# Half of the last stage's joins and norms done on TensorE, ScalarE and GpSimd during the scan (a fused gated block, Trainium2)

## The chip, the cores and the metric

The kernel runs on one core of one Trainium2 chip, as one launch. The metric is the device time of that launch in microseconds; the runs shown are separate executions of the same program. A profile of one further execution gives the trace.

## What is computed

The reference is a chain of four gated pairs, each an attention-like step and a feed-forward step on a residual `x` of 8 batches x 256 tokens x 256 features. The change touches only the last pair:

```python
x = x + tanh(g_xattn[3]) * scan(layernorm(x), ctx)     # _L3_xattn_ref
x = x + tanh(g_ffn[3]) * bit_ffn(layernorm(x), ...)    # _L3_ffn_ref

# scan, for each token t in order, from W = ctx (256 x 256 for each batch), lr = 1/256:
y_t = sigmoid(W @ x_t)
W   = W + lr * (outer(y_t, x_t) - (y_t ** 2)[:, None] * W)

# bit_ffn: ternary weights, activations rounded to 8 bits by the largest |value| of each token
gate = silu(bitlinear(x, w_gate)); up = bitlinear(x, w_up); out = bitlinear(gate * up, w_down)
```

A token's output of the scan depends on all tokens before it. The feed-forward step works on each token alone, so it can start on a token as soon as the scan has passed that token.

## The kernel before

`x` is held in SBUF as 16 row tiles of 128 tokens x 256 features (`core.x`, in profiles `x_res`), two for each batch: tile 2b holds tokens 0 to 127 of batch b, tile 2b+1 tokens 128 to 255. `core.xn` (`x_norm`) holds the normalised rows in the same form.

**The scan** (`scan_steps`, line 2923) runs over 256 tokens in order, all 8 batches at once, with the features on the partitions. W is never formed: the products of tokens with each other are computed before the loop, and for each token VectorE forms the next input `v` from small operations on 16 to 96 columns (lines 3009, 3015, 3046, 3089 and, at the third token of a group of four, 3061 to 3070). ScalarE turns `v` into `y` (line 2983, kept in `y_all`, feature by token) and writes a second copy (line 2987); VectorE cannot go on to the next token's square (line 3024) before that. Tokens form 64 groups m of four (i = 0 to 3). After each group TensorE turns the group's values (line 3148), ScalarE copies them out at i = 1 of the next group (line 2992), TensorE adds products to the accumulators `acc` (lines 3116, 3125), and fills up with idle passes on the identity matrix (line 3134) to a fixed number of passes for each group. GpSimd has nothing to do in this loop. An engine runs its instructions in the order in which its program lists them.

**The last stage** (`stage_tail`, line 3176) takes the 16 row tiles through a pipeline written out by hand: each engine runs turns u = 0 to 23, and in turn u each step works on tile u minus its own lag. The order inside a turn is the order of the `at(...)` calls. The steps, with engine and line of the profile:

- `turn_y` (TensorE, 3242) turns `y_all` to row form; `join` (VectorE, 223 with `tanh_g`) adds it to `x`; `stats` and `mean_var` (VectorE, 3420, 3424); `rstd` (GpSimd, 182 and 185); `normalise` (VectorE, 217).
- `x_range`, `x_cut`, `x_inverse` (VectorE, 3377, 3382, 3386) give the scale of the rounding; `x_scales` (GpSimd, 3449 to 3455); `scale_x` (ScalarE, 3313); `turn_x` (TensorE, 3251); `copy_x` (ScalarE, 3320) takes the turned tile out of PSUM.
- `gate_product` and `up_product` (TensorE, 3261); `gate_silu` (ScalarE, 3329); `product` (VectorE, 3395); `h_range`, `h_scale`, `h_inverse` (VectorE, 3400, 3406, 3411); `h_scales` (GpSimd, 3460, 3462); `scale_h` (ScalarE, 3338); `turn_h` (TensorE, 3279); `copy_h` (ScalarE, 3346); `down` (TensorE, 3289); `leave` (VectorE, 223 with `bt_gate`) adds the result to `x`, and SyncE stores the tile.

`turn_y` and `down` share one PSUM bank. The lags are 0 for the join, 1 for normalise and x_range, 3 for turn_x and copy_x, 4 for the gate and up products, 5 for product and h_range, 6 for turn_h, 7 for down and leave.

`Chain.link` (line 48) gives an instruction a semaphore and makes the engine wait for it before the next one.

## Time and profile before

| | us |
|---|---|
| median of 3 runs | 2042.1 (2037.2 to 2042.43) |
| the profiled execution, its own time | 2038.59 |
| its span in the trace | 2036.9 |
| the scan's loop, start of token 0 to last `y` | about 1669 to 1942 |
| the last stage | about 1943 to 2037 |
| TensorE / VectorE / ScalarE / GpSimd busy over the span | 1865.6 / 1262.3 / 828.5 / 275.4 |

Busy time counts an engine's instructions from start to end, and instructions that follow each other overlap by their latency, so a stretch in which an engine is busy all the time is one in which it never ran dry; how long an instruction keeps the next one waiting is read from start to start. The last 1.7 us between span and time lie outside the trace.

### The profile page before, as it was taken

What the parts mean: (1) busy time and instruction counts of PE and PEld (TensorE: products, weight loads), DVE (VectorE), ACT (ScalarE), POOL (GpSimd) and SP (SyncE); (2) the same over time, 40 slices, a digit from 0 to 9 for tenths busy, and PEclk for the clock granted to TensorE, in tenths of its full rate; (3) what the DMA queues carried; (4) which work ended last, traced back from release to release, by engine and by line L of the source; (5) the groups of instructions that cost most, each with busy time, mean ns of one, the idle gap of its engine ahead of it and who ended that gap; (6) DMA issues with size and microseconds to landing.
All of it is one profiled execution on the core that took longest, in us unless ns stands there. A gap on an engine that the chain in (4) does not pass through costs nothing. (4 is left out here: it accounts for less than half of the span.)

```text
span 2036.9 us, 38837 instructions
## 1 busy us (share of the span) xinstructions
PE 1865.6 (92%) x13683; PEld 1512.2 (74%) x13708; DVE 1262.3 (62%) x4621; ACT 828.5 (41%) x2246; POOL 275.4 (14%) x498
## 2 busy tenths in 40 slices
PE   8899999999998998999999998997983989999978
PEld 6567766777666998999999997776542877777745
DVE  7868876877884361111111145676797539999988
ACT  3434335555563111111111111774486424444468
POOL 2001112000001070000000044332000320000032
PEclk9999999999999998999999999899995989999989
DMA  6211111121112622222222012111000031111100
GB/s 229 89 55 52 43 51 73 46 80 42 42 42 64 244 73 88 88 85 86 87 88 85 23 55 65 45 46 36 29 0 1 0 106 35 36 38 39 24 11 33
DMA packets 106724, 124.98 MB, mean 61 GB/s; under 512 B 36160, under 2 KB 85832, under 8 KB 104776
## 3 DMA queue, kind: packets, MB, share of 16 engines
q1 hardware_dynamic: 95704, 107.64, 15.8%
q0 software_dynamic: 3072, 8.39, 1.3%
q10 hardware_dynamic: 7792, 6.95, 1.0%
q8 instruction: 87, 1.43, 0.3%
q14 instruction: 69, 0.57, 0.1%
HBM read 86.39 MB, written 36.63 MB: 60 GB/s over the span
## 5 line engine op out<-in xcount | busy, mean ns | idle before, releaser
L1804 DVE TENSOR_TENSOR me_h<-me_sg,me_ps_u 128x512 f32<-128x512 f32 x106 | 72.8, 687 | 281.7 <-PE me_ps_u L1615 265.7
L1756 ACT ACTIVATE me_sg<-me_ps_g 128x512 f32<-128x512 f32 x106 | 63.3, 597 | 372.6 <-PE me_ps_g L1615 339.9
L1276 ACT ACTIVATE ca_e<-ca_scored,ca_neg_max 128x256 f32<-128x256 f32 x256 | 127.2, 499 | 108.6 <-DVE ca_neg_max L1335 108.6
L1615 PE MATMUL me_ps_g<-me_x_turned,me_w 128*128 128x128 f32 x1184 | 145.8, 277 | 1.9 <-issue 1.9
L1615 PEld LDWEIGHTS me_ps_g<-me_x_turned,me_w 128*128 128x128 f32 x1184 | 142.1, 193 | 4.3 <-issue 2.1
L1615 PE MATMUL me_ps_u<-me_x_turned,me_w 128*128 128x128 f32 x1184 | 144.5, 275 | 0.0
L1623 PE MATMUL me_ps_y<-me_w,me_h 128*128 128x256 f32 x592 | 140.0, 379 | 0.0
L1615 PEld LDWEIGHTS me_ps_u<-me_x_turned,me_w 128*128 128x128 f32 x1184 | 138.4, 192 | 0.0
L2983 ACT ACTIVATE sc_y_all<-ss_v 128x16 f32<-128x16 f32 x256 | 60.9, 238 | 156.5 <-DVE ss_v L3046 156.4
L1623 PEld LDWEIGHTS me_ps_y<-me_w,me_h 128*128 128x128 f32 x592 | 106.8, 190 | 11.4
L1335 DVE CUSTOM_DVE_ANT_0 ca_scored<-ca_main,ca_mask_add 128x256 f32<-128x256 f32 x256 | 93.0, 422 | 21.5 <-PE ca_main L1219 21.5
L2434 PE MATMUL ig_ps<-nw_int_wT,x_norm 128*128 128x512 f32 (+1 forms) x256 | 90.2, 497 | 0.3 <-ACT if_up L2490 0.3
L3015 DVE SCALAR_TENSOR_TENSOR ss_left<-ss_nq,ss_v 128x16 f32<-128x16 f32 x446 | 90.5, 203 | 0.0
L3134 PE MATMUL ss_idle<-ident 128*128 128x128 f32 x648 | 90.1, 285 | 0.0
L2009 POOL DMA_INDIRECT me_rows<-moe_y_list,me_slot x32 | 31.3, 979 | 429.2 <-DVE carrier L81 421.3
L3134 PEld LDWEIGHTS ss_idle<-ident 128*128 128x128 f32 x648 | 79.4, 195 | 6.3 <-issue 3.2
L2213 ACT ACTIVATE la_e<-la_scores,la_mx 128x128 f32<-128x128 f32 x256 | 70.4, 423 | 33.3 <-DVE la_mx L2255 33.3
L1828 DVE COPY me_y<-me_ps_y 128x256 f32<-128x256 f32 x37 | 15.7, 425 | 108.0 <-PE me_ps_y L1623 108.0
L1231 PE MATMUL ca_turned<-ident,ca_e 128*128 128x128 f32 x512 | 69.3, 279 | 10.6 <-DVE ca_e L1348 10.6
L1231 PEld LDWEIGHTS ca_turned<-ident,ca_e 128*128 128x128 f32 x512 | 57.0, 142 | 27.1 <-DVE ca_e L1348 19.4
L1348 DVE TENSOR_SCALAR ca_e<-ca_e,ca_rsums 128x256 f32<-128x256 f32 x256 | 74.6, 356 | 2.3
L2434 PEld LDWEIGHTS ig_ps<-nw_int_wT,x_norm 128*128 128x128 f32 x256 | 47.1, 194 | 34.0 <-issue 31.7
(451 smaller groups left out, 4365.6 us busy)
## 6 DMA issues: line engine op xcount, KB each, us to landing
me_w<-in_L_ffn_w_e SPq DMA_DIRECT2D x24, 1024.0 KB, 7.7
ca_k_list<-kv_out SPq DMA_DIRECT2D x28, 256.0 KB, 2.3
ca_v_list<-kv_out SPq DMA_DIRECT2D x28, 256.0 KB, 2.3
sk_gb<-scan_g_band SPq DMA_DIRECT2D x14, 512.0 KB, 3.7
moe_x_list<-me_zeros SPq DMA_DIRECT2D x1, 5248.0 KB, 21.8
me_x_tile<-moe_x_list SPq DMA_DIRECT2D x38, 128.0 KB, 2.0
moe_y_list<-me_y ACTq DMA_DIRECT2D x37, 128.0 KB, 1.7
ca_kT<-ca_k_list SPq DMA_DIRECT2D x4, 1024.0 KB, 4.8
```

Source lines behind the costliest of these rows:

```text
L1231: last = nc.tensor.transpose(ps[:, jt * S + it * P:jt * S + (it + 1) * P], e[:, g % 3, e_, it, jt * P:(jt + 1) * P], core.ident[:, :])
L1276: nc.scalar.activation(e[:, g % 3, e_, it, :], scored[:, g % 2, e_, it, :], ACT.Exp, scale=-1.0, bias=neg_max[:, g % 2, n:n + 1], accum_ou ...
L1335: last = nc.vector.tensor_tensor_reduce(scored[:, g % 2, e_, it, :], ps[:, it * S:(it + 1) * S], mask_add[:, b, :], -1.0, -NEG, ALU.add, A ...
L1348: last = nc.vector.tensor_scalar(e[:, g % 3, e_, it, :], e[:, g % 3, e_, it, :], rsums[:, par, n:n + 1], None, ALU.mult)
L1615: last = nc.tensor.matmul(ps[:, j * P:(j + 1) * P], w[:, n, kt, f:f + P], x[:, kt, :], start=(kt == 0), stop=(kt == KD - 1))
L1623: last = nc.tensor.matmul(ps_y[:, 0:D], h[:, c, j, :], w[:, f, :], start=(f == 0), stop=(f == FT - 1))
L1756: nc.scalar.activation(sg[:, c, :], ps_g[c][:, :], ACT.Silu).then_inc(done, 1)
L1804: nc.vector.tensor_tensor(h[:, c, :, :].rearrange("p j n -> p (j n)"), sg[:, c, :], ps_u[c][:, :], ALU.mult).then_inc(done[c], 1)
L2213: last = nc.scalar.activation(e[:, n % 2, r, j, :], scores.ps[r][:, j * P:(j + 1) * P], ACT.Exp, bias=mx[:, n % 2, r, j:j + 1])
L2434: last = nc.tensor.matmul(ps[t % 2][:, lo:hi], xT[:, t, kt * P:(kt + 1) * P], wT[:, w, kt, lo:hi], start=(kt == 0), stop=(kt == KD - 1))
L3015: return nc.vector.scalar_tensor_tensor(out, nq[:, t % 2, :].unsqueeze(2).broadcast_to([P, C, n]), 1.0, src, ALU.add, ALU.mult)
L3134: nc.tensor.matmul(idle[:, 0:P], core.ident[:, :], core.ident[:, :], start=True, stop=True)
```

## The change

The eight tiles that hold tokens 0 to 127 (tile 2b of each batch) are joined and normalised while the scan runs over tokens 128 to 255. It is done in four rounds of two tiles, started at groups 33, 37, 41 and 45. In a round, TensorE turns four 128x128 blocks of `y_all` into a new PSUM bank `ps_f` (`turn_front`), taking the place of four idle passes; ScalarE copies the bank, scaled by `tanh_g`, to a part of SBUF that an earlier stage used (`joined`), after the third token of the group behind; and GpSimd adds it to `x`, takes the mean by folding each row in halves, subtracts it, takes the variance in the same way, and scales: 23 instructions, each waiting for the one before. From the second round on ScalarE's copy also waits until GpSimd is through with the round before.

In the last stage the tiles come in a new order, `tile(t)`: first the eight that are ready, then the other eight. The steps turn_y, join, stats, mean_var, rstd and normalise are done for t = 8 to 15 alone (`at_rest`); the turns begin with u = 1; and `copy_x` goes from ScalarE to VectorE, where it stands behind `leave`.

```diff
@@ -2926,6 +2926,7 @@
     PER = TB // TG
     C = KD * B
     SENT = NG - 2
+    FRONT = tuple(NG // 2 + 1 + 4 * j for j in range(B // 2))
     PASSES = 28
     QUARTER = (0, 1, 0, 1, 2, 3, 0, 1, 0, 1, 2, 3, 0, 1, 2, 3)
     with ExitStack() as ctx:
@@ -2942,6 +2943,12 @@
         ps_z = [st.ps(f"ps_z{j}", [P, 512]) for j in range(2)]
         acc = [st.ps(f"acc{j}", [P, KD, 512]) for j in range(2)]
         idle = st.ps("idle", [P, 512])
+        ps_f = st.ps("ps_f", [P, 2, KD, P])
+        int_wT = core.next_weights.int_wT
+        joined = int_wT[:, 0, 0, 0:2 * D].rearrange("p (n d) -> p n d", n=2)
+        folded = int_wT[:, 0, 1, 0:2 * P].rearrange("p (n k) -> p n k", n=2)
+        mean, rstd = st.sb("mean", [P, 2, 1]), st.sb("rstd", [P, 2, 1])
+        f_ps, f_read, front = st.sem("f_ps"), st.sem("f_read"), Chain(st.sem("front"), 23)
         gb_in = [st.sem(f"gb_in{j}") for j in range(2)]
         gm_in = [st.sem(f"gm_in{n}") for n in range(NBLK)]
         v_ready, y_ready, yz_ready, z_ready = (st.sem(n) for n in ("v_ready", "y_ready", "yz_ready", "z_ready"))
@@ -2991,6 +2998,13 @@
                     act.wait_ge(z_ps, m)
                     nc.scalar.activation(zT[rows, k, :, :].rearrange("p h n -> p (h n)"),
                                          ps_z[(m - 1) % 2][rows, 0:KD * P], ACT.Copy).then_inc(zT_ready, 1)
+                if i == 2 and m - 1 in FRONT:
+                    j = FRONT.index(m - 1)
+                    act.wait_ge(f_ps, j + 1)
+                    if j >= 1:
+                        act.wait_ge(front.sem, front.per * j)
+                    nc.scalar.activation(joined, ps_f[:, :, :, :].rearrange("p n h k -> p n (h k)"), ACT.Copy,
+                                         scale=core.tg[:, 3:4]).then_inc(f_read, 1)
 
         @block.vector
         def _(dve):
@@ -3133,6 +3147,15 @@
                 for _ in range(passes // 2):
                     nc.tensor.matmul(idle[:, 0:P], core.ident[:, :], core.ident[:, :], start=True, stop=True)
 
+            def turn_front(j):
+                pe.wait_ge(y_ready, S // 2)
+                if j >= 1:
+                    pe.wait_ge(f_read, j)
+                for n in range(2):
+                    for h in range(KD):
+                        last = nc.tensor.transpose(ps_f[:, n, h, :], y_all[:, h, 2 * j + n, 0:P], core.ident[:, :])
+                last.then_inc(f_ps, 1)
+
             start_block(0)
             start_block(1)
             for m in range(SENT):
@@ -3170,7 +3193,36 @@
                 for s in share[early:]:
                     whole(ahead, s)
                 real = 12 + 4 * len(share[early:]) + (4 if g < 2 and k + 1 < NBLK else 0)
+                if m in FRONT:
+                    turn_front(FRONT.index(m))
+                    real += 4
                 busy(max(0, PASSES - real))
+
+        @block.gpsimd
+        def _(pool):
+            def fold(link, wide, out):
+
+                link(nc.gpsimd.tensor_tensor(folded[:, :, :], wide[:, :, 0:P], wide[:, :, P:D], ALU.add))
+                n = P // 2
+                while n > 1:
+                    link(nc.gpsimd.tensor_tensor(folded[:, :, 0:n], folded[:, :, 0:n], folded[:, :, n:2 * n], ALU.add))
+                    n //= 2
+                link(nc.gpsimd.tensor_tensor(out, folded[:, :, 0:1], folded[:, :, 1:2], ALU.add))
+
+            for j in range(B // 2):
+                link = front.turn(pool, j).link
+                x, xn = core.x[:, 4 * j:4 * j + 3:2, :], core.xn[:, 4 * j:4 * j + 3:2, :]
+                pool.wait_ge(f_read, j + 1)
+                link(nc.gpsimd.tensor_tensor(x, x, joined[:, :, :], ALU.add))
+                fold(link, x, mean[:, :, :])
+                link(nc.gpsimd.tensor_scalar(mean[:, :, :], mean[:, :, :], 1.0 / D, None, ALU.mult))
+                link(nc.gpsimd.tensor_tensor(xn, x, mean[:, :, :].broadcast_to([P, 2, D]), ALU.subtract))
+                link(nc.gpsimd.tensor_tensor(joined[:, :, :], xn, xn, ALU.mult))
+                fold(link, joined[:, :, :], rstd[:, :, :])
+                link(nc.gpsimd.tensor_scalar(rstd[:, :, :], rstd[:, :, :], 1.0 / D, LN_EPS, ALU.mult, ALU.add))
+                link(nc.gpsimd.tensor_tensor(rstd[:, :, :], rstd[:, :, :],
+                                             core.minus_half[:, :].unsqueeze(1).broadcast_to([P, 2, 1]), ALU.pow))
+                link(nc.gpsimd.tensor_tensor(xn, xn, rstd[:, :, :].broadcast_to([P, 2, D]), ALU.mult))
 
 
 def stage_tail(nc, core, ins, y_all):
@@ -3211,31 +3263,45 @@
         ha_ready, h_ps, hT_ready = st.sem("ha_ready"), st.sem("h_ps"), st.sem("hT_ready")
         out_ps, x_done, stored = st.sem("out_ps"), st.sem("x_done"), st.sem("stored")
         X_SMALL, H_SMALL = 4, 2
-        LAST = 8
+        FIRST, LAST = 1, 8
+        AHEAD = TILES // 2
         block = ctx.enter_context(nc.Block())
 
         def turns(eng_turn):
-            for u in range(TILES + LAST):
+            for u in range(FIRST, TILES + LAST):
                 eng_turn(u)
 
         def at(step, t):
             if 0 <= t < TILES:
                 step(t)
+
+        def at_rest(step, t):
+
+            if AHEAD <= t < TILES:
+                step(t)
+
+        def tile(t):
+
+            return 2 * t if t < AHEAD else 2 * (t - AHEAD) + 1
+
+        def rest(t):
+
+            return t - AHEAD
 
         @block.sync
         def _(sp):
             outs = core.out.rearrange("b (h p) d -> p (b h) d", p=P)
             for t in range(TILES):
                 sp.wait_ge(x_done, t + 1)
-                sp.dma_start(outs[:, t, :], core.x[:, t, :]).then_inc(stored, 16)
+                sp.dma_start(outs[:, tile(t), :], core.x[:, tile(t), :]).then_inc(stored, 16)
             sp.wait_ge(stored, 16 * TILES)
 
         @block.tensor
         def _(pe):
             def turn_y(t):
-                b, half = divmod(t, 2)
-                if t >= 1:
-                    pe.wait_ge(y_added, t)
+                b, half = divmod(tile(t), 2)
+                if rest(t) >= 1:
+                    pe.wait_ge(y_added, rest(t))
                 if t >= 7:
                     pe.wait_ge(x_done, t - 6)
                 for h in range(KD):
@@ -3282,7 +3348,8 @@
 
             def down(t):
                 pe.wait_ge(hT_ready, 2 * t + 2)
-                pe.wait_ge(y_added, min(TILES, t + 7))
+                if rest(t + 7) >= 1:
+                    pe.wait_ge(y_added, rest(min(TILES, t + 7)))
                 if t >= 1:
                     pe.wait_ge(x_done, t)
                 for f in range(FT):
@@ -3296,7 +3363,7 @@
                 at(down, u - 7)
                 at(turn_h, u - 6)
                 at(up_product, u - 4)
-                at(turn_y, u)
+                at_rest(turn_y, u)
 
             turns(turn)
 
...
-            def copy_x(t):
-                act.wait_ge(x_ps, t + 1)
...
-                at(copy_x, u - 3)
...
+            def copy_x(t):
+                dve.wait_ge(x_ps, t + 1)
+                if t >= 2:
+                    dve.wait_ge(up_ps, 2 * (t - 1))
+                nc.vector.tensor_scalar(xT[:, t % 2, :, :].rearrange("p k n -> p (k n)"), ps_x[:, 0:D], MAGIC, None,
+                                        ALU.subtract).then_inc(xT_ready, 1)
+
             def join(t):
-                dve.wait_ge(y_ps, t + 1)
-                residual(nc, dve, core, tg, ps_yo[:, 0:D], t, y_added)
+                dve.wait_ge(y_ps, rest(t) + 1)
+                residual(nc, dve, core, tg, ps_yo[:, 0:D], tile(t), y_added)
 
             def normalise(t):
-                norm.vector_apply(dve, t, t % 2)
+                dve.wait_ge(norm.rstd_ready, rest(t) + 1)
+                nc.vector.tensor_scalar(core.xn[:, tile(t), :], core.x[:, tile(t), :], norm.mv[:, t % 2, 0:1],
+                                        norm.rstd[:, t % 2:t % 2 + 1], ALU.subtract, ALU.mult).then_inc(norm.done, 1)
 
             def x_range(t):
-                dve.wait_ge(norm.done, t + 1)
-                nc.vector.tensor_reduce(xmax[:, t:t + 1], core.xn[:, t, :], AX.X, ALU.max, apply_absolute_value=True
+                if t >= AHEAD:
+                    dve.wait_ge(norm.done, rest(t) + 1)
+                nc.vector.tensor_reduce(xmax[:, t:t + 1], core.xn[:, tile(t), :], AX.X, ALU.max, apply_absolute_value=True
                                         ).then_inc(xmax_ready, 1)
 
...
             def turn(u):
                 at(product, u - 5)
                 at(leave, u - 7)
+                at(copy_x, u - 3)
                 at(h_range, u - 5)
-                at(normalise, u - 1)
+                at_rest(normalise, u - 1)
                 at(h_scale, u - 5)
                 at(x_range, u - 1)
                 at(h_inverse, u - 5)
-                at(join, u)
+                at_rest(join, u)
                 at(x_cut, u - 1)
-                at(stats, u)
+                at_rest(stats, u)
                 at(x_inverse, u - 1)
-                at(mean_var, u)
+                at_rest(mean_var, u)
...
```

How the order of the instructions moves: first TensorE in the scan, group m = 33 (`ss_ps_f` is the new PSUM bank, `ss_idle` the idle passes; the line numbers of the change are higher). Before:

```order
L3116 MATMUL ss_acc<-sk_gm,ss_zT 128x128 x2
L3125 MATMUL ss_acc<-sk_gm,ss_zT 128x8x4 x2
L3125 MATMUL ss_acc<-sk_gm,ss_zT 128x128 x2
L3134 MATMUL ss_idle<-ident 128x128 x6
L3148 MATMUL ss_ps_z<-ident,ss_z 32x128 x2
```

And with the change:

```order
L3130 MATMUL ss_acc<-sk_gm,ss_zT 128x128 x2
L3139 MATMUL ss_acc<-sk_gm,ss_zT 128x8x4 x2
L3139 MATMUL ss_acc<-sk_gm,ss_zT 128x128 x2
L3156 MATMUL ss_ps_f<-ident,sc_y_all 128x128 x4
L3148 MATMUL ss_idle<-ident 128x128 x4
L3171 MATMUL ss_ps_z<-ident,ss_z 32x128 x2
```

The four transposes stand behind the group's products, and two idle multiplications (four passes) are gone.

ScalarE beside it, with the change (`nw_int_wT` is the SBUF part that holds `joined`); before, the same rows stand there without L3006:

```order
L2999 ACTIVATE ss_zT<-ss_ps_z 32x256
L2990 ACTIVATE sc_y_all<-ss_v 128x16
L2994 ACTIVATE ss_az<-ss_v 128x16
L3006 ACTIVATE nw_int_wT<-ss_ps_f,tanh_g 128x512
L2990 ACTIVATE sc_y_all<-ss_v 128x16
L2994 ACTIVATE ss_az<-ss_v 128x16
```

The copy stands between the third and the fourth token of the group: the fourth token's `y` is queued behind it.

VectorE in the last stage, one full turn before (u = 7 and later), from leave on:

```order
L223 SCALAR_TENSOR_TENSOR x_res<-bt_ps_yo,bt_gate,x_res 128x256
L3400 TENSOR_REDUCE bt_hmax<-bt_hp 128x1
L217 TENSOR_SCALAR x_norm<-x_res,bt_ln_mean_var,bt_ln_rstd 128x256
L3406 TENSOR_SCALAR bt_hsc<-bt_hmax,bt_cgu 128x1
L3377 TENSOR_REDUCE bt_xmax<-x_norm 128x1
```

and with the change the same place for u = 7, the last turn without join and norm:

```order
L3465 TENSOR_TENSOR bt_hp<-bt_sg,bt_ps_u 128x512 x2
L223 SCALAR_TENSOR_TENSOR x_res<-bt_ps_yo,bt_gate,x_res 128x256
L3432 TENSOR_SCALAR bt_xT<-bt_ps_x 128x256
L3470 TENSOR_REDUCE bt_hmax<-bt_hp 128x1
L3476 TENSOR_SCALAR bt_hsc<-bt_hmax,bt_cgu 128x1
L3447 TENSOR_REDUCE bt_xmax<-x_norm 128x1
L3481 RECIPROCAL bt_hinv<-bt_hsc 128x1
L3452 TENSOR_SCALAR bt_xs<-bt_xmax 128x1
L3456 RECIPROCAL bt_xr<-bt_xs 128x1
```

The norm has left the turn, and the copy out of PSUM (L3432) has come into it; from u = 8 on the join and its statistics, and from u = 9 on the norm, are back, and the copy stays.

## Rows read from the trace of the kernel before

**Rows 1.** Stretches: length; PE, PEld, DVE, ACT, POOL busy us (count); PEclk; DMA share; GB/s.
```profile
1696.90:1917.90 221.00, 205.66 (x1460) 169.61 (x1460) 216.93 (x1610) 93.69 (x467) 0.00 (x0) 1.00 0.15 37
1971.05:2008.16 37.11, 34.82 (x222) 22.49 (x225) 37.11 (x106) 37.11 (x66) 13.88 (x64) 1.00 0.09 30
```
**Rows 2.** Timeline around group 33: start us, us, engine, line, form, idle before.
```profile
1817.55 0.22 ACT L2987 ACTIVATE ss_az<-ss_v 128x16 f32<-128x16 f32 x1
...
1818.32 1.60 PE L3134 MATMUL ss_idle<-ident 128*128 128x128 f32 x12
1818.42 0.24 ACT L2983 ACTIVATE sc_y_all<-ss_v 128x16 f32<-128x16 f32 x1 [0.65 <-DVE ss_v L3046]
...
1818.70 0.19 DVE L3024 SCALAR_TENSOR_TENSOR ss_nq<-sc_y_all 128x16 f32<-128x16 f32 x1
```
**Rows 3.** Timeline of GpSimd: a wide addition undisturbed, small operations of the last stage.
```profile
324.90 0.72 POOL L1378 TENSOR_TENSOR x_res<-x_res,kv_bias 128x256 f32 x1
2004.73 0.19 POOL L3450 TENSOR_TENSOR bt_xs<-bt_xs,bt_amax_inv 128x1 f32<-128x1 f32 x1
2005.00 0.19 POOL L3452 TENSOR_TENSOR bt_cgu<-nw_bit_scale,bt_xs 128x2 f32<-128x2 f32 x1
2005.68 0.55 POOL L185 TENSOR_TENSOR bt_ln_rstd<-bt_ln_rstd,minus_half 128x1 f32<-128x1 f32 x1
```
**Rows 4.** VectorE line 1348, 128x256 from SBUF to SBUF: beside GpSimd, alone, and beside it in time.
```profile
L1348 DVE TENSOR_SCALAR ca_e<-ca_e,ca_rsums x4: 347/348/353, 421.0 to 421.8; 128x256 f32<-128x256 f32 x4
326.43 0.82 DVE L1348 TENSOR_SCALAR ca_e<-ca_e,ca_rsums 128x256 f32<-128x256 f32 x1
327.17 0.81 DVE L1348 TENSOR_SCALAR ca_e<-ca_e,ca_rsums 128x256 f32<-128x256 f32 x1
```
**Rows 5.** A small GpSimd operation beside VectorE operations on two SBUF tensors (timeline), and its group.
```profile
146.53 0.74 POOL L182 TENSOR_TENSOR f_ln_rstd<-f_ln_mean_var,eps 128x1 f32<-128x1 f32 x1 [12.02 <-DVE f_ln_mean_var L176]
146.36 0.86 DVE L671 SCALAR_TENSOR_TENSOR f_qh_down<-f_qh_above,f_qh_up 128x704 f32<-128x704 f32 x1
L182 POOL TENSOR_TENSOR f_ln_rstd<-f_ln_mean_var,eps x14: 742/744/746, 146.5 to 302.5; 128x1 f32<-128x1 f32 x14
```
**Rows 6.** Timeline of the start of the last stage, the steps on the way to the first product.
```profile
1943.56 0.21 DVE L3365 TENSOR_SCALAR bt_c_out<-tanh_g,nw_bit_scale 128x1 f32<-128x1 f32 x1
1947.94 0.15 DVE L3386 RECIPROCAL bt_xr<-bt_xs 128x1 f32<-128x1 f32 x1
1949.86 0.47 ACT L3320 ACTIVATE bt_xT<-bt_ps_x,bt_magic 128x256 bf16<-128x256 f32 x1 [0.78 <-PE bt_ps_x L3251]
1953.56 1.49 PE L3261 MATMUL bt_ps_g<-nw_bit_wT,bt_xT 128*128 128x512 bf16 x3 [0.22 <-issue]
1954.84 1.87 PE L3261 MATMUL bt_ps_u<-nw_bit_wT,bt_xT 128*128 128x512 bf16 x4
1958.78 1.27 DVE L3395 TENSOR_TENSOR bt_hp<-bt_sg,bt_ps_u 128x512 f32<-128x512 f32 x2
```
**Rows 7.** VectorE in the last stage: the groups of the four moved steps, and two timeline rows.
```profile
L223 DVE SCALAR_TENSOR_TENSOR x_res<-bt_ps_yo,tanh_g,x_res 128x256 f32<-128x256 f32 x16 | 7.5, 470 | 0.3 <-PE bt_ps_yo L3242 0.3
L3420 DVE BATCH_NORM_STATS2 bt_ln_stats<-x_res 128x6 f32<-128x256 f32 x16 | 6.8, 427 | 0.0
L217 DVE TENSOR_SCALAR x_norm<-x_res,bt_ln_mean_var,bt_ln_rstd 128x256 f32<-128x256 f32 x16 | 6.5, 408 | 5.8 <-POOL bt_ln_rstd L185 5.8
L3424 DVE BATCH_NORM_AGGREGATE bt_ln_mean_var<-bt_ln_stats 128x2 f32<-128x6 f32 x16 | 2.9, 182 | 0.0
1984.97 0.47 DVE L223 SCALAR_TENSOR_TENSOR x_res<-bt_ps_yo,tanh_g,x_res 128x256 f32<-128x256 f32 x1
1985.35 0.14 DVE L3382 TENSOR_SCALAR bt_xs<-bt_xmax 128x1 f32<-128x1 f32 x1
```
**Rows 8.** ScalarE's turn of the last stage, timeline around the copy that moves.
```profile
1991.42 0.45 ACT L3320 ACTIVATE bt_xT<-bt_ps_x,bt_magic 128x256 bf16<-128x256 f32 x1
1991.78 1.25 ACT L3329 ACTIVATE bt_sg<-bt_ps_g,bt_cgu 128x512 f32<-128x512 f32 x2
```

21 lines of the change are left out of this document (9 added, 12 removed).

## The prediction

> **What bounds the kernel now.** The busy time by stretch comes first, since the change has two places. In the scan's loop VectorE is busy for 216.93 of 221.00 us, ScalarE for 93.69, GpSimd not at all [rows 1]; 52 groups of four tokens pass in that stretch, 4.25 us each. VectorE alone sets this pace. In the last stage's full turns VectorE and ScalarE are both busy all the time, 37.11 of 37.11 us for eight turns, 4.64 us a turn [rows 1]; there the reader is to see two engines close to the bound. The timeline of the stage's start then shows a long filling: from VectorE's first own operation at 1943.56 to the first product at 1958.78 it takes 15.2 us, in which join, statistics, GpSimd's root and norm follow each other for every tile [rows 6]. VectorE waits 5.8 us for GpSimd's root there [rows 7].
>
> All sums are made against the profiled execution (2038.59). It lies 3.5 us under the median of the three runs and 2.0 under their mean (2040.6); I add the net difference to that mean. From run to run some 0.3% (6 us) is about what a measurement of this kernel can tell from no change.
>
> **The change part by part.**
>
> *The filling gets shorter.* For the first tiles VectorE starts with x_range at once, about 1943.7; x_cut and x_inverse follow within 0.6 us, so x_inverse of tile 0 starts near 1944.3 instead of 1947.94. From there to the copy out of PSUM it took 1949.86 - 1947.94 = 1.9 us [rows 6], so copy_x(0) stands near 1946.2. It lasts 0.47, the second tile's transpose (waiting for it) some 0.7, so gate_product(0) starts near 1947.4. From the gate product to the up product it took 1.28 us [rows 6], and half of the up product's 1.87 is needed: first product near 1949.6 instead of 1958.78. Gain 9.2 us.
>
> *Turns without join and norm.* u = 5 to 7 lose join, stats, normalise and mean_var: durations 470, 427, 408 and 182 ns, each keeping the next one 0.09 us less than it lasts (join: 1985.35 - 1984.97 = 0.38) [rows 7], together 1.13 us. ScalarE loses copy_x, 1991.78 - 1991.42 = 0.36 us [rows 8]; VectorE gets it at about the same 0.36. VectorE's turn would be 4.64 - 1.13 + 0.36 = 3.9, ScalarE's 4.64 - 0.36 = 4.3 at most. Some leaves wait for `down` in these turns; I take 0.5 us of gain for the three.
>
> *Full turns.* u = 8 to 15 keep everything and VectorE, already full, gets copy_x: 8 x 0.36 = 2.9 us lost. The last turns, where ScalarE was late, give back about 0.6. Last stage: -9.2 - 0.5 + 2.9 - 0.6 = **-7.4 us**, between -4 (copy waits for turn_x, filling saves only 6) and -11 (full turns at 4.64, because the copy fills gaps).
>
> *TensorE.* Four transposes stand in place of two idle multiplications. L3134's row of 12 lasts 1.60 us, 0.13 each [rows 2]: four transposes take some 0.55. They can start at 1818.32, where the idle passes begin, and nobody waits for the idle passes: nothing, except as the start of the next point.
>
> *ScalarE's copy in front of a `y`.* ScalarE is free from about 1817.77 (L2987's end) and would wait for the transposes to 1818.95; the copy reads 128x512 from PSUM, as bt_sg does, 1.25 us for two [rows 8], so about 0.6 until the next instruction starts. The fourth token's `y` then starts at 1819.6 instead of 1818.42. Behind it is L3024, which started 0.04 us after that `y` ended [rows 2], and behind that all of VectorE. No slack: 1.2 us a round, **+4.8 us** for four; nothing if the copy somehow slips into a gap, 7 if the transposes come later.
>
> *GpSimd's 23 chained instructions.* A 128x256 addition lasts 0.72 us and a one-column one 0.19 [rows 3], so 2.07 ns a column; a dependent one starts 0.08 us after the end of the one before (2004.73 + 0.19 to 2005.00). A round has four operations of 512 columns and two folds of 256, 128, 64, 32, 16, 8, 4 and 2: 3068 columns, 6.4 us. With 23 x 0.27 and 0.36 more for the power (0.55 against 0.19) a round takes 13.0 us. Rounds begin four groups apart, 17.0 us. They fit, with 4 us to spare, and GpSimd's own time is hidden.
>
> *What GpSimd's operations cost VectorE.* This decides. L1348, 128x256 from SBUF to SBUF, lasts 0.35 us and follows itself every 0.27 us (421.0 to 421.8 for four). Beside GpSimd's 128x256 additions it lasts 0.81 and follows itself every 327.17 - 326.43 = 0.74 us [rows 4]: the two engines take turns, and VectorE loses 0.47 us for each GpSimd operation of 256 columns, two thirds of that operation. Does that hold for the scan's VectorE operations, which mostly read two SBUF tensors and have no such twin here? One direction is seen: a one-column GpSimd operation lasts 0.74 instead of 0.19 us, and ends at 147.27, just behind VectorE's L671 (146.36 + 0.86 = 147.22), an operation on two SBUF tensors; 14 of 14 do so [rows 5]. The two exclude each other then, and I take it that they do in the other order too. At 0.47 us for 256 columns a round's wide operations (4 x 512, 2 x 448) hold VectorE for 5.4 us; the narrow ones (under 64 columns) fit between two VectorE starts and cost nothing; and each of some ten wide ones begins while VectorE could not have started anyway, 0.08 us each. That is 4.6 us a round, **+18.3 us** for four. The bounds are 0 (two-tensor reads are not held) and 4 x 10.8 = 43 (GpSimd's whole durations, 23 x 0.19 + 6.4 a round).
>
> The Trainium skill, "SBUF — State Buffer", section "Who interferes with whom", says that a VectorE instruction with two SBUF inputs contends with a GpSimd instruction that reads SBUF, and that the one that issues second is blocked until the first has finished. The trace agrees for the one order, and its 0.47 of 0.72 us says that the block is shorter than the recorded duration. By the page's words alone the sum would be near the upper bound.
>
> **Sum:** +18.3 + 4.8 - 7.4 = +15.7 us; 2040.6 + 15.7 = 2056.3, said as **2056**. The moved work is small for VectorE in the last stage (8 x 1.13 = 9 us, of which 5.8 come back as copies), and about 2.6 times as much is asked of VectorE in waiting.
>
> **The rivals.**
> - *VectorE isn't held.* For: no row of before shows a two-tensor VectorE operation behind a GpSimd one. Against: the turns that the two take, and GpSimd's wait for L671 [rows 4, 5]. Then +4.8 - 7.4 = -2.6: 2038. Chance 0.15.
> - *Faster: VectorE isn't held, and the shorter filling carries the whole stage.* The same without the hold, with the last stage at its -11: +4.8 - 11 = -6.2 or better: 2034. It decides by the first product: if that comes within 5.5 us of the stage's start and the full turns stay at 4.64, this case is there. For: ScalarE's copy is only moved, and VectorE has small waits for its own results to fill. Against: VectorE is at 37.11 of 37.11. Chance 0.14.
> - *Held for GpSimd's whole duration.* A VectorE operation behind a GpSimd one waits until that has ended, in small operations too: +43 + 4.8 - 7.4 = +40: 2081. Against it is the 0.47 of 0.72 us [rows 3, 4]. Chance 0.05. This is the rule of the Trainium skill's page "SBUF — State Buffer" taken word for word.
> - *GpSimd falls behind.* If VectorE's dense stream holds GpSimd off for a VectorE duration (0.2 us) at each of 23 links and more, a round grows from 13.0 to 18 us and beyond the spacing; ScalarE then waits for the round in front of a `y`, and the scan stands. The spacing itself grows to about 22 us with the hold, so it takes 9 us of waits in a round. Then 3 x 5 = 15 us more: 2071. Chance 0.06.
>
> **How the numbers follow.** The forecast has 0.60, the rivals 0.15, 0.14, 0.05 and 0.06. The forecast's own range is 2044 to 2067 (hold 9 to 27 us, last stage -4 to -11). To hold 8 in 10 the range goes down over the first rival and the nearer part of the second, to 2034, and up to 2068; the two dear rivals stay out. Faster by over 0.3% (under 2036): the second rival, 0.14. Within 0.3%: the first, and a sliver of the forecast, 0.18. Slower: 0.68.
>
> **What would show it.** In the stretch of groups 34 to 49 VectorE's groups last longer than 4.25 us while GpSimd has wide operations, and 4.25 in its pauses; single VectorE rows there of 0.5 to 1.2 us beside wide GpSimd rows, where 0.19 to 0.25 stood. L3006 starts about 1.2 us after L2994's end and the next `y` right behind it. From ScalarE's first L3006 to GpSimd's last instruction of the round 13 to 18 us. The first product within 5.5 to 6.5 us of the last stage's start, turns near 4.2 first and 5.0 from u = 8 on. Wrong is the forecast if VectorE rows beside GpSimd stay at 0.19 to 0.25 us, or if the loop's length hardly grows; then the hold was misread. If the loop grows by over 30 us, the hold is priced too low.

## The result, and the profile after

The changed kernel takes 2057.9 us, the median of four runs (2057.09 to 2058.5), beside 2041.9 for the kernel before on the same chip (2037.2 to 2042.43): a ratio of 1.0088, 95% interval 1.0076 to 1.0101. It is slower by 0.9%.

The windows view by stretch divides it. First the kernel after; the columns are those of [rows 1]. The first stretch is the scan's loop, from VectorE's first `ss_z` row to its last (one row a group, so their starts also give each group's period); the second is the last stage, from VectorE's first constant to the end of the span.

```profile
1670.58:1960.65 290.07, 258.81 (x1712) 214.09 (x1712) 276.47 (x1892) 112.53 (x554) 44.46 (x92) 0.93 0.13 32
1969.39:2055.35 85.96, 69.70 (x424) 42.93 (x432) 73.19 (x198) 70.53 (x113) 22.09 (x112) 0.96 0.08 26
```

The same two stretches of the kernel before:

```profile
1672.69:1935.03 262.34, 244.35 (x1712) 201.59 (x1712) 255.29 (x1891) 110.26 (x550) 0.00 (x0) 0.99 0.14 35
1943.44:2036.86 93.42, 73.73 (x440) 45.30 (x448) 77.04 (x214) 76.32 (x129) 27.81 (x128) 0.92 0.07 24
```

The loop grew by 290.07 - 262.34 = 27.7 us, the last stage shrank by 93.42 - 85.96 = 7.5. The loop began 2.1 us earlier in this execution (nothing of the change lies ahead of it), and the way from loop to stage took 0.3 longer: 27.7 - 7.5 - 2.1 + 0.3 = 18.5, which is the spans' difference (2036.9 to 2055.4). VectorE's count in the loop is the same but for one, yet it was busy for 21.2 us more: its instructions lasted longer. The remaining 6.5 us of the loop are idle time of VectorE.

The timeline of the first round (group 33; before is [rows 2]) shows both kinds. L2990 is now the line of the `y`, L3006 ScalarE's new copy, L3216 GpSimd's first addition, L3038 the first VectorE instruction behind a `y`:

```profile
1815.52 0.22 ACT L2994 ACTIVATE ss_az<-ss_v 128x16 f32<-128x16 f32 x1
1816.99 0.69 ACT L3006 ACTIVATE nw_int_wT<-ss_ps_f,tanh_g 128x512 f32<-128x512 f32 x1 [1.25 <-PE ss_ps_f L3156]
1817.57 0.23 ACT L2990 ACTIVATE sc_y_all<-ss_v 128x16 f32<-128x16 f32 x1
1817.76 1.26 POOL L3216 TENSOR_TENSOR x_res<-x_res,nw_int_wT 128x512 f32<-128x512 f32 x1 [174.87 <-ACT nw_int_wT L3006]
1817.83 1.22 DVE L3038 SCALAR_TENSOR_TENSOR ss_nq<-sc_y_all 128x16 f32<-128x16 f32 x1 [1.08 <-ACT sc_y_all L2990]
1818.98 0.21 DVE L3084 TENSOR_TENSOR ss_v<-ss_left,ss_far 128x64 f32<-128x64 f32 x1
...
1819.25 0.74 DVE L3029 SCALAR_TENSOR_TENSOR ss_left<-ss_nq,ss_v 128x64 f32<-128x64 f32 x1
```

First VectorE stands idle for 1.08 us, because the `y` waited behind the copy (L2994's end at 1815.74, the copy not before 1816.99). Then a 16-column instruction, 0.19 us before [rows 2], lasts 1.22: it began 0.07 us after GpSimd's 512-column addition and the next VectorE start comes at 1818.98, just ahead of that addition's end at 1819.02. The same a little later, away from ScalarE's copy:

```profile
1822.89 1.11 POOL L3219 TENSOR_TENSOR x_norm<-x_res,ss_mean 128x512 f32<-128x512 f32 x1
1822.91 0.19 DVE L3038 SCALAR_TENSOR_TENSOR ss_nq<-sc_y_all 128x16 f32<-128x16 f32 x1
1823.01 1.09 DVE L3023 TENSOR_TENSOR ss_adds<-sk_gb,sc_y_all 128x80 f32<-128x80 f32 x1
1824.02 0.18 DVE L3029 SCALAR_TENSOR_TENSOR ss_left<-ss_nq,ss_v 128x16 f32<-128x16 f32 x1
```

L3038 is not held here, though GpSimd's row began 0.02 us ahead of it; L3023, 0.24 us when alone, takes 1.09. GpSimd's groups, seen over the loop (busy us, mean ns | idle before), say that its own rows are hardly longer than the 2.07 ns a column of the prediction (0.19 + 512 x 2.07 ns = 1.25):

```profile
L3216 POOL TENSOR_TENSOR x_res<-x_res,nw_int_wT 128x512 f32<-128x512 f32 x4 | 5.0, 1261 | 208.8 <-ACT nw_int_wT L3006 208.8
L3219 POOL TENSOR_TENSOR x_norm<-x_res,ss_mean 128x512 f32<-128x512 f32 x4 | 4.2, 1058 | 0.3
L3205 POOL TENSOR_TENSOR nw_int_wT<-x_res 128x256 f32<-128x256 f32 x4 | 3.3, 816 | 0.3
```

Group periods, which were 4.25 us before, show where the rounds are: 7.14, 6.83, 5.12, 4.45 us in the first round (that last group takes 4.46 before, too), 8.13, 7.01, 4.99, 4.24 in the second; the third is like the first, and the fourth, which begins with 8.34, like the second. A GpSimd round takes 13.0 us in the first and 12.8 in the other three; in its pause a group is back at 4.24. The waits of the loop that are new, VectorE's for a `y`, ScalarE's for the four transposes and for a turned `z` (us in total, times, longest):

```profile
DVE ss_nq L3038 <- ACT sc_y_all L2990: 6.2, 6, 1.4
ACT nw_int_wT L3006 <- PE ss_ps_f L3156: 5.6, 4, 1.6
...
ACT ss_zT L2999 <- PE ss_ps_z L3171: 2.3, 4, 1.1
```

TensorE's granted clock changed too. Before, it is 1.00 over all of these groups [rows 1]; after the change it is 0.50, the lower of its two levels (1.2 instead of 2.4 GHz), in parts of every round. The windows view over GpSimd's first round:

```profile
1817.76:1830.77 13.01, 9.33 (x46) 7.62 (x46) 12.80 (x56) 3.41 (x18) 11.25 (x23) 0.74 0.16 43
```

TensorE waits longer for VectorE's slower groups (22.2 us in all for `ss_z` from 1800 on, 8.6 before) and is busy for 9.33 of 13.01 us here (205.66 of 221.00 before [rows 1]), at a mean clock of 0.74. In two groups this comes back to VectorE. With the clock at 0.50 from 1835.6 to 1839.0 and from 1883.4 to 1886.8, ScalarE gets the turned `z` 0.85 and 1.06 us late, and VectorE waits 0.50 and 0.70 us for the `y` behind it and then 1.4 us, not 1.1, for the one behind the copy. These are the groups of 8.13 and 8.34 us that stand where the other two rounds have 7.14 and 7.20, some 1.9 us of waiting in all.

The last stage, to be laid beside [rows 6]: the way to the first product, and then one full turn.

```profile
1969.39 0.06 DVE L3420 MEMSET bt_magic<- 128x1 f32 x1 [1.92 <-PEq L95]
...
1969.64 0.41 DVE L3447 TENSOR_REDUCE bt_xmax<-x_norm 128x1 f32<-128x256 f32 x1
...
1972.28 0.42 DVE L3432 TENSOR_SCALAR bt_xT<-bt_ps_x 128x256 bf16<-128x256 f32 x1 [1.14 <-PE bt_ps_x L3317]
...
1975.98 1.28 DVE L3465 TENSOR_TENSOR bt_hp<-bt_sg,bt_ps_u 128x512 f32<-128x512 f32 x2 [1.31 <-ACT bt_sg L3390]
```

```profile
2002.84 1.28 DVE L3465 TENSOR_TENSOR bt_hp<-bt_sg,bt_ps_u 128x512 f32<-128x512 f32 x2
2004.04 0.48 DVE L223 SCALAR_TENSOR_TENSOR x_res<-bt_ps_yo,bt_gate,x_res 128x256 f32<-128x256 f32 x1
2004.44 0.41 DVE L3432 TENSOR_SCALAR bt_xT<-bt_ps_x 128x256 bf16<-128x256 f32 x1
2004.77 1.21 DVE L3470 TENSOR_REDUCE bt_hmax<-bt_hp 128x1 f32<-128x1024 f32 x1
```

From the stage's start to the first product it takes 6.6 us (15.3 before). The copy out of PSUM, now VectorE's, keeps the next instruction 2004.77 - 2004.44 = 0.33 us, and the next product comes at 2007.81: a full turn of 4.97 us where 4.64 stood.

### The profile page after: what moved, and what is told of

Same layout as the page of the kernel before. It is cut to its first block and busy times, and to the rows that moved or that the text cites. A ratio compares the mean times of both kernels' runs of the same rounds, so it can differ in the third digit from the quotient of the medians.

```text
span 2055.4 us, 38859 instructions
## 1 busy us (share of the span) xinstructions
PE 1872.6 (91%) x13667; PEld 1519.4 (74%) x13692; DVE 1277.5 (62%) x4605; ACT 825.3 (40%) x2234; POOL 313.2 (15%) x574
## 3 DMA queue, kind: packets, MB, share of 16 engines
q1 hardware_dynamic: 95704, 107.64, 15.7%
q10 hardware_dynamic: 7792, 6.95, 1.0%
## 5 line engine op out<-in xcount | busy, mean ns | idle before, releaser
L2990 ACT ACTIVATE sc_y_all<-ss_v 128x16 f32<-128x16 f32 x256 | 60.8, 238 | 173.7 <-DVE ss_v L3060 173.5
L3029 DVE SCALAR_TENSOR_TENSOR ss_left<-ss_nq,ss_v 128x16 f32<-128x16 f32 x446 | 96.3, 216 | 0.0
L1828 DVE COPY me_y<-me_ps_y 128x256 f32<-128x256 f32 x37 | 15.7, 424 | 108.1 <-PE me_ps_y L1623 108.1
L1348 DVE TENSOR_SCALAR ca_e<-ca_e,ca_rsums 128x256 f32<-128x256 f32 x256 | 73.0, 349 | 2.2
L3130 PE MATMUL ss_acc<-sk_gm,ss_zT 128*128 128x128 f32 x420 | 72.2, 315 | 0.0
```

The source lines that it names most:

```text
L1348: last = nc.vector.tensor_scalar(e[:, g % 3, e_, it, :], e[:, g % 3, e_, it, :], rsums[:, par, n:n + 1], None, ALU.mult)
L3029: return nc.vector.scalar_tensor_tensor(out, nq[:, t % 2, :].unsqueeze(2).broadcast_to([P, C, n]), 1.0, src, ALU.add, ALU.mult)
L3130: nc.tensor.matmul(acc[n % 2][:, h, 0:P], zT[:, k, h, :], gm[:, gram_pair(n, k), :, :].rearrange("p b t -> p (b t)"), start=False, stop=Tr ...
```

## The experiments

**The theory:** the loop's growth is GpSimd's wide operations holding VectorE's two-tensor ones, some 18 us, and ScalarE's copy ahead of a `y`, some 5. **Rivals:** the growth comes from the copy and TensorE's transposes (ScalarE or TensorE late, VectorE only waits); GpSimd's mere activity (its starts and signals) disturbs, not its reads; many small holds and not the wide ones. A further rival, TensorE late at its lower clock, had no run of its own, but the traces price it. Five kernels leave part of the work out: e1 everything of GpSimd in the scan (ScalarE's copy is made and nobody uses it); e2 the transposes and the copy (GpSimd joins what lies in the buffer); e3 has zeros written in place of GpSimd's operations; e7 keeps of them only those of up to 32 columns for each of the two tiles, e8 their number and widths but each with one input.

**e1: GpSimd left out**

```diff
-                    if j >= 1:
-                        act.wait_ge(front.sem, front.per * j)
...
-        @block.gpsimd
-        def _(pool):
...
-                link(nc.gpsimd.tensor_tensor(xn, xn, rstd[:, :, :].broadcast_to([P, 2, D]), ALU.mult))
```

> Leaves out GpSimd's part of the rounds: the first eight tiles keep the x and the norm of the stage before; the transposes, ScalarE's copies and the whole last stage stay. The loop's length is read from the first to the last ss_z row of VectorE: 262.3 us before the change, 290.1 with it (+27.8). Theory A (GpSimd's operations hold VectorE's two-tensor operations off for about 21 us, ScalarE's copy in front of a y costs 1.4 to 1.6 us a round): the loop comes to 268 to 269 us, the whole to 21 us under the changed kernel, about 2036. Theory B (the growth comes from ScalarE's copy, the transposes and the semaphores, GpSimd beside it is free): the loop stays above 285 us. The last stage stays at 86 us under both, against 93.4 before.

Measured: 2036.5 us against 2037.2, ratio 0.9994 (0.9984 to 1.0004). Its loop:

```profile
1672.13:1940.38 268.25, 247.38 (x1712) 204.49 (x1712) 255.06 (x1892) 112.57 (x554) 0.00 (x0) 0.97 0.14 35
```

The loop is 268.2 us, 5.9 over before and 21.8 under after, and VectorE's busy time is back at 255. The last stage keeps its gain (86.2). Of the 5.9, 4.3 are the four groups with ScalarE's copy (5.32 us each instead of 4.25). The other 1.6 are two later groups of 5.06 and 5.23 us, where TensorE brings `z` late. The timeline there:

```profile
1844.66 0.62 PE L3169 MATMUL ss_ps_z<-ident,ss_z 128*32 128x128 f32 x4
1845.32 0.38 ACT L2999 ACTIVATE ss_zT<-ss_ps_z 32x256 f32<-32x256 f32 x1 [1.08 <-PE ss_ps_z L3169]
...
1845.99 0.20 DVE L3036 SCALAR_TENSOR_TENSOR ss_nq<-sc_y_all 128x16 f32<-128x16 f32 x1 [0.72 <-ACT sc_y_all L2990]
```

ScalarE waits 1.08 us for the turned `z`, and the `y` behind it makes VectorE wait 0.72. The trace also has the reason why this `z` is late. TensorE's granted clock is 0.50 from 1840.8 to 1844.2 (and from 1878.3 to 1881.7, at the other late group), and the 16 products ahead of the `z` take 3.39 us. In e3, at a clock of 1.00, the same 16 take 2.05. First e1, its clock over part of the row and the row; then the row of e3:

```profile
1841.40:1843.40 2.00, 2.00 (x10) 2.00 (x10) 1.96 (x15) 0.72 (x4) 0.00 (x0) 0.50 0.00 0
1841.34 3.39 PE L3128 MATMUL ss_acc<-sk_gm,ss_zT 128*128 128x128 f32 x16
1839.84 2.05 PE L3130 MATMUL ss_acc<-sk_gm,ss_zT 128*128 128x128 f32 x16
```

Ahead of the fall TensorE had stood idle for 1.38 us, behind the group with the copy. The run e3 has the same 1.38 us and keeps its clock, so why it falls in the one execution and not in the other stays open. The kernel before also has two groups a little longer than 4.25 us (4.46 and 4.43), but there ScalarE never waits for a `z`.

**e2: GpSimd alone, without transposes and copy**

```diff
-                if i == 2 and m - 1 in FRONT:
...
-                if m in FRONT:
-                    turn_front(FRONT.index(m))
-                    real += 4
...
-                pool.wait_ge(f_read, j + 1)
+                pool.wait_ge(y_ready, TG * FRONT[j] + TG + 3)
```

> Leaves out the transposes and ScalarE's copies; GpSimd's four rounds of 23 instructions run on what lies in the buffers, each started by the y of the same token. Theory A: the loop grows by about 21.5 us over 262.3, to 283 to 285, with VectorE rows of up to 1 us beside the wide GpSimd rows. Theory B: it stays within 2 us of 262.3.

Measured in one run: 2055.6 us (before 2037.2).

```profile
1673.26:1958.91 285.65, 261.08 (x1712) 216.66 (x1712) 276.79 (x1892) 110.17 (x550) 44.01 (x92) 0.92 0.13 33
```

The loop is 285.7 us: 23.3 over before, with nothing changed on ScalarE and TensorE. A typical round has groups of 6.17, 6.96 and 5.06 us, so 5.4 us beyond 3 x 4.25, in each of the four. One round has 1.5 more: its first group takes 7.69 us, with the granted clock at 0.50 all through it and ScalarE waiting 1.68 us for `z`. The 5.4 us do not hang on the clock: the second groups of the four rounds take 6.95 to 6.98 us at mean clocks of 0.50, 0.54, 0.75 and 0.76. e1 and e2 together (5.9 + 23.3 = 29.2) make more than the 27.7 of the whole change, because each has some 1.5 us of its own of a `z` late at the lower clock. Without these, 4.3 for the copies and 21.6 for GpSimd, with the 1.9 of late `z` in the changed kernel itself, make 27.8. The rival "ScalarE and TensorE" falls: it has 6 of 28 us.

**e3: GpSimd only writes**

```diff
+                for _ in range(times):
+                    link(nc.gpsimd.memset(out, 0.0))
...
-                link(nc.gpsimd.tensor_tensor(x, x, joined[:, :, :], ALU.add))
-                fold(link, x, mean[:, :, :])
...
+                fill(link, joined[:, :, :], 2)
+                fold(link)
```

> As the changed kernel, but each GpSimd instruction of the rounds is a memset of the same target columns (the wide ones twice), 29 in a round: GpSimd writes SBUF and reads nothing; the first eight tiles keep the x and the norm of the stage before. Theory A in its narrow form (the hold comes from GpSimd's reads): the loop comes to 268 to 269 us, as without GpSimd. Theory C (GpSimd holds VectorE off whenever it uses SBUF at all, writes too): about 8 us of fills in each round of wide and narrow operations show as 5 to 15 us more, the loop above 273.

Measured in one run: 2033.4 us. The loop, and the timeline at a wide write:

```profile
1671.16:1937.53 266.37, 244.29 (x1712) 201.48 (x1712) 254.84 (x1892) 112.49 (x554) 30.14 (x116) 0.99 0.14 35
```

```profile
1821.42 0.19 DVE L3038 SCALAR_TENSOR_TENSOR ss_nq<-sc_y_all 128x16 f32<-128x16 f32 x1
1821.51 0.52 POOL L3206 MEMSET nw_int_wT<- 128x512 f32 x1
1821.53 0.24 DVE L3023 TENSOR_TENSOR ss_adds<-sk_gb,sc_y_all 128x80 f32<-128x80 f32 x1
```

GpSimd is busy for 30.14 us in 116 chained instructions, and the loop is 266.4, only the 4.0 over before that ScalarE's copies cost. That is 1.6 under the expected range, which was taken from e1's length: here the clock stays at 1.00, and there is no late `z`. L3023 beside a 512-column write stays at 0.24 us where it took 1.09 beside a 512-column subtraction. So neither GpSimd's activity nor its writing holds VectorE: its reading does. The Trainium skill's page "SBUF — State Buffer", section "Who interferes with whom", says the same, that a VectorE instruction with two SBUF inputs contends with a GpSimd instruction that reads SBUF, not with one that only writes it; this run agrees, 4.0 us against 27.7.

**e4: ScalarE's copy behind the last `y` of the group**

```diff
-                if i == 2 and m - 1 in FRONT:
+                if i == 3 and m - 1 in FRONT:
```

> ScalarE's copy of a round stands one token later, behind the group's fourth y, where ScalarE waited 0.92 us for VectorE in any case. Theory A: the waits of VectorE for a y (6.2 us in the loop) go to under 1 us, the loop shrinks by 5 to 6 us to about 284.5, the whole to about 2052. If the 1.4 us a round is not the place of the copy but a wait that only shows there (the hold of GpSimd begins at the same moment), the loop stays within 1 us of 290.1.

Measured: 2056.7 us against 2037.2, ratio 1.0087 (1.0062 to 1.0113). The loop, and the wait for the `y` that was 6.2 us after the change:

```profile
1672.89:1960.26 287.37, 258.47 (x1712) 214.40 (x1712) 276.38 (x1892) 112.55 (x554) 45.65 (x92) 0.93 0.13 32
```

```profile
DVE ss_nq L3038 <- ACT sc_y_all L2990: 2.1, 3, 0.8
```

The loop is 2.7 us shorter than after, where 5 to 6 were expected. VectorE waits 4.1 us less for `y`, and 1.4 of that come back elsewhere. None of the waits that are left is at a copy: the four of the copies (5.0 of the 6.2 us) are gone, and the three here (0.56, 0.75 and 0.81 us) stand behind a `z` that came 1.05 to 1.30 us late, each at the end of a stretch with the clock at 0.50. VectorE's busy time is the same, 276.4. So moving the copy gave 2.7 us of the 28, net; what it would give with the clock at 1.00 is not measured. The ratio against before cannot be told from the change's own.

**e5: the copy of the last stage back on ScalarE**

```diff
+            def copy_x(t):
+                act.wait_ge(x_ps, t + 1)
...
+                nc.scalar.activation(xT[:, t % 2, :, :].rearrange("p k n -> p (k n)"), ps_x[:, 0:D], ACT.Identity,
+                                     bias=magic[:, 1:2]).then_inc(xT_ready, 1)
...
+                at(copy_x, u - 3)
```

> The changed kernel with copy_x back on ScalarE, at its old place in the turn. Read from the start of the last stage to the span's end: 93.4 us before, 86.0 with the change. If copy_x on VectorE is what stretches the full turns from 4.64 to 4.97 us, these go back to 4.64 (2.6 us less over eight turns), while the first turns, 3.65 us with the change, go to about 4.5, since ScalarE's turn is that long (2.6 us more over three). The last stage stays within 1.5 us of 86. If the longer full turns have another cause, they stay at 4.97 and the stage gets longer than 87.5 us. The loop stays at 288 to 291 us.

Measured in one run: 2060.2 us (before 2041.9). The last stage:

```profile
1973.52:2058.48 84.96, 69.75 (x424) 43.56 (x432) 68.16 (x182) 75.50 (x129) 22.16 (x112) 0.94 0.08 26
```

The stage is 85.0 us instead of 86.0. Its full turns are back at 4.64 from the third on; the first two take 5.29 and 4.76, so that the eight together are 1.8 us shorter, not 2.6. Its first product comes at 1980.79, after 7.3 us instead of 6.6. That is the copy's place too: with it on VectorE the seven other runs of that form (e1 to e4, e6 to e8) take 6.5 to 6.8 us, with it on ScalarE e9 and e10 take 7.1 and 7.3. The three light turns (12.1 us, 12.0 with the change) and the end (27.7) are as they were; the expected light turns of 4.5 us did not come. The time as a whole is no lower, since this execution's loop took 291.1 (one group of 6.16 us in it has a `z` 2.1 us late, at a clock of 0.50): a microsecond of the last stage is below what one run can tell.

**e6: the statistics on ScalarE, only one-column work on GpSimd**

TensorE joins in PSUM (`x` through the identity, then the transposed `y` through an identity times the gate), for one tile at a time. ScalarE copies out with a running sum, squares with a running sum, and later makes the norm; GpSimd has six instructions of one column for a tile.

```diff
-    FRONT = tuple(NG // 2 + 1 + 4 * j for j in range(B // 2))
+    FRONT = (33, 35, 37, 39, 41, 43, 45, 49)
...
+                    nc.scalar.activation(core.x[:, 2 * j, :], ps_f[:, 0:D], ACT.Copy,
+                                         accum_out=sums[:, j:j + 1]).then_inc(f_read, 1)
+                    nc.scalar.activation(junk, ps_f[:, 0:D], ACT.Square, accum_out=sumsq[:, j:j + 1]).then_inc(f_read, 1)
+                if i == 2 and m - 3 in FRONT:
...
+                    nc.scalar.activation(core.xn[:, 2 * j, :], core.x[:, 2 * j, :], ACT.Identity,
+                                         scale=rstd[:, j:j + 1], bias=off[:, j:j + 1])
...
+                nc.tensor.matmul(ps_f[:, 0:D], core.ident[:, :], core.x[:, 2 * j, :], start=True, stop=True,
+                                 skip_group_check=True)
```

> The same work with no wide GpSimd operation: TensorE adds x and the scaled, turned y in PSUM (one tile at a time, groups 33, 35 and so on), ScalarE takes x and its sum, then the squares' sum, behind the fourth y of the next group, and the norm behind the third y two groups later; GpSimd does six one-column operations a tile. The last stage is the changed one. Theory A: only one-column operations are left to hold VectorE, and ScalarE's operations of 0.4 to 0.5 us lie where it waited 0.65 to 0.92 us for VectorE: the loop comes to 262.5 to 266 us (262.3 before, 290.1 with the change), the last stage stays near 86, and the whole is 4 to 7 us under the kernel before, about 2032. If the loop grows because the eight tiles' work is in it at all, whatever the engine, it stays above 275.

Measured: 2035.9 us against 2041.9, ratio 0.9967 (0.9951 to 0.9982).

```profile
1676.95:1941.64 264.69, 246.02 (x1714) 203.06 (x1714) 255.70 (x1891) 119.61 (x590) 13.65 (x48) 0.99 0.14 35
1950.07:2036.22 86.15, 70.03 (x424) 43.13 (x432) 73.28 (x198) 70.49 (x113) 22.13 (x112) 0.96 0.08 26
```

The same work beside the same scan costs 2.4 us instead of 27.7 (the clock is 1.00 in all these groups, and no `z` is late), and the last stage keeps its gain: the idea of the change holds, its engine was the wrong one. VectorE's busy time is what it was before. The rest is in five of the eight tiles, where a group takes 4.75 us instead of 4.25 and VectorE waits 0.37 us for a `y`.

**e7: only the narrow ones of GpSimd's operations**

```diff
-                link(nc.gpsimd.tensor_tensor(folded[:, :, :], wide[:, :, 0:P], wide[:, :, P:D], ALU.add))
-                n = P // 2
+                n = P // 4
...
-                link(nc.gpsimd.tensor_tensor(xn, x, mean[:, :, :].broadcast_to([P, 2, D]), ALU.subtract))
-                link(nc.gpsimd.tensor_tensor(joined[:, :, :], xn, xn, ALU.mult))
```

> GpSimd alone as in the run with neither transposes nor copies, and of its 23 operations only the 15 of 64 columns and fewer, on what lies in the buffers. The prediction took these for free: then the loop is 262 to 263.5 us. If each of the 60 holds VectorE for 0.08 us or more, which would close the gap between the forecast 18.3 us of hold and the measured 23.3, it is 267 or more.

Measured in one run: 2032.6 us (before 2041.9).

```profile
1672.22:1936.18 263.96, 244.47 (x1712) 201.66 (x1712) 256.74 (x1891) 110.28 (x550) 16.91 (x60) 0.99 0.15 35
```

60 operations cost 1.6 us of loop, 0.4 a round, 0.03 each on average; the VectorE rows that got longer by over 0.06 us are all beside those of 64 and 32 columns. The rival of the many small holds falls: of e2's 5.4 us a round the eight wide operations have 5.0.

**e8: GpSimd's operations with one input each**

```diff
+                link(nc.gpsimd.tensor_scalar(out, src, 1.0, None, ALU.mult))
...
-                link(nc.gpsimd.tensor_tensor(x, x, joined[:, :, :], ALU.add))
+                one(link, joined[:, :, :], core.x[:, 4 * j:4 * j + 3:2, :])
```

> GpSimd alone, 23 operations of the same target columns, each reading one SBUF tensor instead of two (a multiplication by a constant), on what lies in the buffers. With two inputs the loop grew by 23.3 us. If the hold is GpSimd's reading, it goes by what it reads and how long: with half the reading and shorter operations the loop grows by 8 to 15 us, to 270 to 278. If only operations with two inputs hold, it stays within 2 us of 262.3.

Measured in one run: 2043.6 us (before 2041.9). The loop, and the timeline at a wide one:

```profile
1675.38:1946.96 271.58, 247.15 (x1712) 204.32 (x1712) 263.76 (x1891) 110.33 (x550) 53.58 (x92) 0.97 0.14 34
```

```profile
1820.27 1.54 POOL L3195 TENSOR_SCALAR nw_int_wT<-x_res 128x512 f32<-128x512 f32 x1 [173.35 <-ACT sc_y_all L2990]
1820.35 0.66 DVE L3016 TENSOR_TENSOR ss_adds<-sk_gb,sc_y_all 128x80 f32<-128x80 f32 x1
1820.93 0.18 DVE L3022 SCALAR_TENSOR_TENSOR ss_left<-ss_nq,ss_v 128x16 f32<-128x16 f32 x1
```

The loop grows by 9.2 us where 92 two-input operations made it 23.3 (e2). Of the 9.2, 0.8 is one group behind the last round, with a `z` 1.04 us late at a clock of 0.50. A 512-column operation with one input lasts longer (1.54 us instead of 1.04 to 1.26) and holds a VectorE instruction for about half as long: 0.66 - 0.24 = 0.42 us, and the next VectorE start comes while GpSimd still has 0.9 us to go. So the price does not go by the length of GpSimd's rows. That it goes by the number of reads is the likely reading and not shown: a multiplication by a constant is also another kind of instruction than an addition of two tensors.

**e9: e6, with the squares' sum moved and the last stage's copy back on ScalarE** (e5's edit added to e6, and in the scan the squares' sum behind the first `y` of the next group)

```diff
-                    nc.scalar.activation(junk, ps_f[:, 0:D], ACT.Square, accum_out=sumsq[:, j:j + 1]).then_inc(f_read, 1)
+                if i == 0 and m - 2 in FRONT:
+                    j = FRONT.index(m - 2)
+                    nc.scalar.activation(junk, ps_f[:, 0:D], ACT.Square, accum_out=sumsq[:, j:j + 1]).then_inc(f_read, 1)
...
+                at(copy_x, u - 3)
```

> The kernel whose rounds run on TensorE and ScalarE, with two edits: the squares' sum of a tile moves from right behind the first PSUM read to behind the first y of the next group (before, the two reads together made VectorE wait 0.50 us in five of the eight tiles), and copy_x is back on ScalarE (the stage was 85.0 instead of 86.0 us with it there). Loop 262.4 to 263 us (was 264.7), last stage 85 to 85.5 us; the whole 3 to 4 us under that kernel and 9 to 10 under the kernel before. If the waits were TensorE's, late in the group, and not two reads in a row, the loop stays at 264.5.

Measured: 2031.5 us against 2039.4, ratio 0.9962 (0.995 to 0.9975), nine runs of 2027.0 to 2037.2.

```profile
1672.72:1940.86 268.14, 251.73 (x1714) 208.06 (x1714) 256.58 (x1892) 120.36 (x590) 12.99 (x48) 0.96 0.14 35
1949.32:2033.88 84.56, 69.69 (x432) 42.97 (x432) 68.09 (x182) 75.63 (x129) 22.18 (x112) 0.96 0.08 26
```

The last stage takes 84.6 us, 1.6 less than e6's. In this execution the loop's first groups, long before any of the added work, took 4.6 us more than usual (6.96, 7.43 and 5.03 us instead of 6.1, 4.5 and 4.25). The granted clock is 0.50 up to 1693.3 here, 20 us into the loop, and in the kernel before up to 1680.1. Without these 4.6 us the loop is 263.6, as in e10, whose scan is the same. The squares' sum moved takes the 4.75 us groups of e6 to 4.4, with no wait for a `y` left.

**e10: e9, with the remaining eight norms on GpSimd**

```diff
-                at_rest(normalise, u - 1)
...
+                nc.gpsimd.tensor_scalar(core.xn[:, tile(t), :], core.x[:, tile(t), :], norm.mv[:, t % 2, 0:1],
+                                        norm.rstd[:, t % 2:t % 2 + 1], ALU.subtract, ALU.mult).then_inc(norm.done, 1)
```

> As the one before, and the norm of the second eight tiles, 128x256, goes from VectorE to GpSimd in the last stage. Theory A (only VectorE operations with two SBUF tensors, or plain SBUF to SBUF ones, are held by GpSimd): the VectorE operations left in this stage read PSUM or one SBUF tensor, so none of its large rows gets longer; VectorE's full turn falls from 4.64 to 4.3 us and ScalarE's 4.53 sets it, 0.5 to 1 us less in all. Rival (any wide GpSimd operation holds VectorE): 0.47 us for each of the eight, full turns of 4.8 us, 1.3 us more.

Measured: 2031.5 us against 2039.4, ratio 0.9965 (0.9952 to 0.9978).

```profile
1668.51:1932.11 263.60, 246.35 (x1714) 203.24 (x1714) 256.07 (x1891) 119.96 (x590) 12.92 (x48) 0.98 0.14 35
1940.55:2025.45 84.90, 70.35 (x432) 43.56 (x432) 66.95 (x174) 75.43 (x129) 31.95 (x120) 0.94 0.08 26
```

The groups view of its last stage (mean ns of one), GpSimd's new operation and the two large ones of VectorE that run beside it:

```profile
L3528 POOL TENSOR_SCALAR x_norm<-x_res,bt_ln_mean_var,bt_ln_rstd 128x256 f32<-128x256 f32 x8 | 9.8, 1230 | 0.8
...
L3462 DVE TENSOR_REDUCE bt_hmax<-bt_hp 128x1 f32<-128x1024 f32 x16 | 19.4, 1211 | 0.1
L223 DVE SCALAR_TENSOR_TENSOR x_res<-bt_ps_yo,bt_gate,x_res 128x256 f32<-128x256 f32 x16 | 7.7, 484 | 9.3 <-PE bt_ps_yo L3352 9.1
```

GpSimd reads SBUF for 9.8 us here, and VectorE's rows keep their lengths (1211 ns, as 1.21 us in the full turn above; 484 beside 481 in e9). Both read one large operand from SBUF at most: the maximum's only one, and of the two of `leave` the other comes from PSUM. One operand alone does not make an instruction safe, though: L1348 of [rows 4] reads one tensor from SBUF, writes to SBUF, and was held. The only large instruction of that kind in this stage was the norm, which has gone to GpSimd, so this run does not try one. The turns go from 4.64 to 4.56 us and no further, since ScalarE is now busy for 4.56 of 4.56 us; the end takes the rest back. By their ratios against before e6, e9 and e10 cannot be told apart; they are the best versions measured, 0.3 to 0.4% under it.

## Why the prediction was right

The forecast was 2056, the measured median 2057.9, by the mechanism that was forecast: GpSimd's wide reads hold VectorE, ScalarE's copy delays a `y`, and the last stage gives back less than they cost. That the number came as near as 1.9 us is partly luck, as the last point says. By its own steps, in the profiled executions (the loop's terms from e1 and e2):

| step | forecast | measured |
|---|---|---|
| hold of VectorE, four rounds | +18.3 | +21.6 (4 x 5.4, e2) |
| ScalarE's copy ahead of a `y` | +4.8 | +4.3 (4 x 1.07, e1) |
| TensorE late with `z` | none | +1.6 (e1) |
| way to the first product | -9.2 | -8.7 |
| three light turns | -0.5 | -1.3 |
| eight full turns | +2.9 | +2.6 |
| end of the stage | -0.6 | +0.05 |
| sum | +15.7 | +20.2 |

- **The hold** was 3.3 us too small. The argument from [rows 4, 5] stood: two engines that take turns, in one order seen and in the other inferred. The rate stood as well: at 0.47 us for 256 columns the prediction had 5.4 us a round, and e2 has 5.4. What was mis-sized is the 0.08 us taken off for each wide operation, on the ground that it begins while VectorE could not have started (the four rounds then come to 18.4; it says 18.3). It priced the operations of 512, 256 and 128 columns at 0.86, 0.39 and 0.16 us; over the four rounds of the changed kernel the VectorE rows beside them are longer by 0.90, 0.51 and 0.25 on average. The two single rows shown above grew by 0.85 (1.09 from 0.24) and 1.03 us (1.22 from 0.19). And the narrow ones, priced at nothing, cost 0.4 us a round with those of 64 columns (e7).
- **ScalarE's copy** came as predicted, a `y` later by its wait and its length. L3006 started 1.25 us after L2994's end, as the list of signs had it.
- **TensorE's lateness** was missed: the prediction costed the four transposes at nothing but the start of the next point. The two late groups of e1 come two groups behind the second and the fourth copy, and e3, with the same transposes and copies, does not have them. The difference is the granted clock: 0.50 where the `z` is late in e1 (16 products in 3.39 us), 1.00 in e3 (2.05 us). The prediction left TensorE's clock out. What the changed kernel itself pays for it is some 1.9 us, in its second and fourth round. Why the clock falls in one execution and not in another is not shown.
- **The last stage** came out at -7.5 for a forecast of -7.4, which is luck: errors of up to 0.8 us in its terms cancel. The first product came 6.6 us after the start where 6.0 was computed (5.5 to 6.5 in the list of signs), so the filling gave 0.5 us less. The light turns were 3.63, 3.65 and 4.72 us (12.0 for three, against 13.3 before) where 4.2 was forecast: the limit taken for ScalarE, 4.64 - 0.36, does not hold in the first turns (probably since its steps on `h` only join from u = 6 on). And the end, which was to give 0.6 back, took 27.7 us as before.
- **The rivals.** "Not held" and "faster" fall by the rows of 1.09 and 1.22 us. "Held for the whole duration" falls by its price, 43 us of hold against 21.6. The block is close to GpSimd's duration for a single operation of 512 columns with two inputs (1.03 of 1.26 us), some three quarters of it for the wide ones together (20 of 27 us: e2 less e7), and about half in all (21.6 of the 44 us that GpSimd is busy in e2). So the rule that the prediction names for this rival does not hold to the letter here. "GpSimd falls behind" falls by rounds of 12.8 to 13.0 us, the 13.0 of the forecast.
- **The number.** The loop's sum was 4.6 us too low, and the median only 1.9. The difference is the executions' own: the loop of the profiled run after began 2.1 us earlier, and the profiled run of before lay 2 us under the mean that the sum was added to. As a difference of medians the change costs 16.0 us, as one of profiled executions 18.5; the mechanism's size is known to about 2 us, no better.

## What to carry to other kernels

An idle engine is not a free one: ask what the added work shares with the engine that bounds the stretch. Beside a VectorE that lives on instructions with two tensors in SBUF, GpSimd work that reads two wide tensors costs about three quarters of its own length; writes, narrow operations, and the same sums on ScalarE cost little or nothing, as e3, e7 and e6 show. Before moving work, look in the trace of before for the one place where both engines run at once and read how the rows change: the rate of [rows 4], 0.47 us for 256 columns, gave the price to within a tenth once nothing was taken off it. And before a wait for TensorE is put down to an edit, lay the granted clock of the same window beside that of the other run: here every `z` that came late did so beside a clock of 0.50.

## What the runs showed of the hardware that was not expected

- GpSimd's memsets, 512 columns in 0.52 us, ran beside a full VectorE with no effect (e3), while a 512-column subtraction made a 0.24 us instruction last 1.09.
- With one input in place of two GpSimd's row is longer (1.54 us for 512 columns, 1.04 to 1.26 with two) and the hold shorter, some 0.42 us instead of 0.85 to 1.03 (e8).
- A VectorE instruction that starts within 0.02 us of GpSimd's row can still pass unhindered, and the next one is held (1822.91 and 1823.01 above).
- In the last stage, where VectorE's large instructions beside them take one large operand from SBUF at most, eight GpSimd operations of 1.23 us left its rows unchanged (e10).
- TensorE's granted clock fell to 0.50 in the middle of a loop in which it had been 1.00, in executions in which TensorE had waited more than before (0.74 on average in GpSimd's first round, TensorE busy for 9.33 of 13.01 us); e3, which waits more too, keeps 1.00. Where a `z` was then late it cost 0.8 to 1.7 us of loop each time (e1, e2, e5); the other falls cost nothing that shows.
